# Residual tiles of the attention output projection: from 64 loads of 256 KB into scratch tiles to 16 loads of 1 MB into the query tile

## The reference

```python
x = x + attn(layernorm(x), wq, wk, wv, wo)     # attn ends in  y @ wo
x = x + ffn(layernorm(x), w_gate, w_up, w_down)
```

## Time and profile before

| what | value |
|---|---|
| time before, median of 3 runs | 6593.12 us (6577.72 to 6980.12) |
| the profiled execution's own time | 6586.74 us |
| its span (core 2, the slowest) | 6585.2 us |
| spans of the 8 cores | 6537.8 to 6585.2 us |
| PE busy, share of the span | 5290.5 us, 80% |
| output projection loops of the four slots, core 2 | 541.6 us in sum |

### The profile page before, as it was taken

The page is one execution under the profiler, slowest core; times in us unless marked ns, Lnnn a source line. Parts: engine busy times, 40 slices in busy tenths (PEclk is TensorE's granted clock), DMA queues, the critical chain, the costliest instruction groups (busy, mean ns, idle before and its releaser), DMA issues. The chain is left out here.

```text
span 6585.2 us, 56999 instructions; the slowest of 8 cores (6537.8 to 6585.2 us)
## 1 busy us (share of the span) xinstructions
PE 5290.5 (80%) x21360; PEld 2023.8 (31%) x21360; DVE 996.9 (15%) x1236; ACT 1358.1 (21%) x1451; POOL 310.4 (5%) x382
## 2 busy tenths in 40 slices
PE   5777767647874788558986399999999998888997
PEld 1222222112221222212222144444444443443443
DVE  1222223124112410041000100000000000000000
ACT  1222213312541366115662000000000000000000
POOL 0000000000000000000000010011111110000000
PEclk8777778667886888878887699999999998999999
DMA  7445412022012200310002466666666666667774
GB/s 107 67 74 88 67 37 48 28 86 67 1 32 88 61 1 1 99 56 13 1 1 80 103 96 96 96 96 96 96 96 96 96 96 161 223 230 226 234 233 166
DMA packets 581435, 599.36 MB, mean 91 GB/s; under 512 B 343601, under 2 KB 454194, under 8 KB 581170
## 3 DMA queue, kind: packets, MB, share of 16 engines
q0 software_dynamic: 346016, 272.65, 25.6%
q1 hardware_dynamic: 235154, 323.06, 15.4%
HBM read 625.02 MB, written 125.83 MB: 114 GB/s over the span
## 5 line engine op out<-in xcount | busy, mean ns | idle before, releaser
L1251 PE MATMUL pDa<-gld,wdl 128*128 128x512 bf16 x4096 | 904.7, 385 | 141.9 <-DVE ost L1265 110.4
L1128 PE MATMUL pG<-ln2T,wgb 128*128 128x512 bf16 x4096 | 896.8, 380 | 79.3 <-DMA wub<-wuT 79.3
L1141 PE MATMUL pU<-ln2T,wub 128*128 128x512 bf16 x4096 | 894.5, 379 | 0.0
L880 ACT ACTIVATE probs<-pS,kbb,rsc 128x1024 bf16<-128x1024 f32 (+3 forms) x640 | 729.8, 1140 | 502.0 <-PE pS L853 318.9
L1251 PEld LDWEIGHTS pDa<-gld,wdl 128*128 128x128 bf16 x4096 | 404.7, 99 | 641.9 <-issue 172.0
L1128 PEld LDWEIGHTS pG<-ln2T,wgb 128*128 128x128 bf16 x4096 | 400.9, 98 | 566.0 <-issue 84.0
L1141 PEld LDWEIGHTS pU<-ln2T,wub 128*128 128x128 bf16 x4096 | 401.2, 98 | 482.9
L982 PE MATMUL pY<-lyT,wqb 128*128 128x512 bf16 x1024 | 293.0, 457 | 249.9 <-DMA wqb<-scr_wo 236.1
L894 PE MATMUL pR<-probs,selb 128*1 128x512 bf16 (+3 forms) x1280 | 380.6, 380 | 92.8 <-ACT probs L880 48.0
L1150 ACT ACTIVATE silo<-pG 128x2048 f32<-128x2048 f32 x64 | 120.1, 1877 | 1621.0 <-PE pG L1128 1621.0
L1153 DVE TENSOR_TENSOR gst<-silo,pU 128x2048 bf16<-128x2048 f32 x64 | 146.4, 2288 | 1681.5 <-PE pU L1141 1681.5
(11 more groups left out here) (115 smaller groups left out, 2598.3 us busy)
## 6 DMA issues: line engine op xcount, KB each, us to landing
gld<-scr_gated SPq DMA_DIRECT2D x64, 1024.0 KB, 6.8
wdl<-scr_wd SPq DMA_DIRECT2D x64, 1024.0 KB, 12.3
wdl<-scr_wd POOLq DMA_DIRECT2D x64, 1024.0 KB, 11.2
wgb<-wgT POOLq DMA_DIRECT2D x64, 512.0 KB, 8.6
wub<-wuT POOLq DMA_DIRECT2D x64, 512.0 KB, 15.8
wds<-wdT POOLq DMA_DIRECT2D x64, 512.0 KB, 17.1
scr_wd<-wds SPq DMA_DIRECT2D x64, 512.0 KB, 10.3
scr_gated<-gst SPq DMA_DIRECT2D x64, 512.0 KB, 9.8
```

The lines of the kernel that those rows point to most:

```text
L880: rcol=rcol: e.activation(A(probs[g2], noff, [[1024, 128], [512, 2], [1, 512 - noff]]), A(pS[g2], noff, [[1024, 128], [512, 2], [1, 512 - ...
L1128: ctx.op("tensor", lambda e, dk=dk, gi=gi, buf=buf: e.matmul(pG[:, gi * 512:(gi + 1) * 512], wgb[buf][:, dk * 128:(dk + 1) * 128], ln2T[:, ...
L1141: ctx.op("tensor", lambda e, dk=dk, gi=gi, buf=buf: e.matmul(pU[:, gi * 512:(gi + 1) * 512], wub[buf][:, dk * 128:(dk + 1) * 128], ln2T[:, ...
L1251: pD=pD: e.matmul(pD[:, dki * 512:(dki + 1) * 512], wdl[buf][:, hci * DSW + dki * 128: hci * DSW + dki * 128 + 128], gld[buf][:, hci * 512 ...
```

## The change

Three things are edited, all in `ph_slots`.

- The residual is loaded four blocks at a time, in 4 loads of 1 MB per slot (128 partitions x 4 x 512 f32) and not in 16 of 256 KB. They go into `xr4v`, a view of `qT` as f32 with two halves of 4 blocks, which alternate. The load of a group is issued by SP at the first block of the group (`dk` 0, 4, 8, 12) and stands ahead of that block's weight load. It waits for the last addition that read its half and for the end of attention (`yev`, and `avp` for the first two groups of a slot).
- The waits that guarded `roq0` and `roq1` against residual loads go (one before each rotation, one before the copy in attention); each write of `qT` (L809) gets waits for the residual loads instead.
- In the statistics, a square waits for the casts of its own two blocks and not for that of block 15, and each matmul on `xbq` waits for the cast of its own block; before, only the first had a wait.

```diff
             qT = asb("qT", [128, NH * 512], BF16)
+            xr4v = qT.bitcast(F32)
...
-            xr0 = roq0
-            xr1 = roq1
...
                         ctx.op("vector", lambda e, x1=x1, ro=ro: e.tensor_mul(ro[0:64, :], x1, csq[:, :]),
-                               waits=[("tm", mq["proj"][qc]), ("d_cs", m_cs),
-                                      (f"d_xr{qc % 2}", ctx.c(f"d_xr{qc % 2}"))])
+                               waits=[("tm", mq["proj"][qc]), ("d_cs", m_cs)])
...
                             qT[:, qc * 512:(qc + 1) * 512], ro[:, :], pY[:, 0:512]),
-                            waits=[("tm", m_rqb)])
+                            waits=[("tm", m_rqb),
+                                   ("d_xr0", ctx.c("d_xr0")), ("d_xr1", ctx.c("d_xr1"))])
...
                             ctx.op("vector", lambda e: e.tensor_copy(roq0[:, :], pR[:, 0:512]),
-                                   waits=[("tm", m_rb), ("d_xr0", ctx.c("d_xr0"))])
+                                   waits=[("tm", m_rb)])
...
+                    m_xr4 = {}
                     for dk in range(DK):
                         buf = dk % 2
+                        NXR = min(4, (NH * 256) // 1024)
+                        HWID = NXR * 512
+                        g4 = dk // NXR
+                        if dk % NXR == 0:
+                            xb4 = g4 % 2
+                            ctx.op("sync", lambda e, g4=g4, xb4=xb4, slot=slot: e.dma_start(
+                                out=A(xr4v, xb4 * HWID, [[NH * 256, 128], [512, NXR], [1, 512]]),
+                                in_=A(dram["xqT"].tensor, g4 * NXR * 128 * OWN + slot * 512,
+                                      [[OWN, 128], [128 * OWN, NXR], [1, 512]])),
+                                waits=[("vm", max(mk["xres_v"][xb4], mk["yev"])),
+                                       ("tm", mk["avp"] if g4 < 2 else 0),
+                                       (f"d_xr{xb4}", ctx.c(f"d_xr{xb4}"))],
+                                inc=f"d_xr{xb4}", n=16)
+                            m_xr4[g4] = ctx.c(f"d_xr{xb4}")
                         ctx.op("sync" if buf == 0 else "gp", lambda e, dk=dk, buf=buf: e.dma_start(
...
-                        ctx.op("sync", lambda e, dk=dk, buf=buf, slot=slot: e.dma_start(
-                            out=xr[buf][:, :],
-                            in_=A(dram["xqT"].tensor, dk * 128 * OWN + slot * 512,
-                                  [[OWN, 128], [1, 512]])),
-                            waits=[("vm", max(mk["xres_v"][buf], mk["yev"])),
-                                   (f"d_xr{buf}", ctx.c(f"d_xr{buf}"))], inc=f"d_xr{buf}", n=16)
-                        m_xr = ctx.c(f"d_xr{buf}")
+                        m_xr = m_xr4[g4]
...
-                            o1f[buf][:, :], pO, xr[buf][:, :]),
-                            waits=[("tm", m_o1), (f"d_xr{buf}", m_xr),
+                            o1f[buf][:, :], pO,
+                            xr4v[:, (g4 % 2) * HWID + (dk % NXR) * 512:(g4 % 2) * HWID + (dk % NXR) * 512 + 512]),
+                            waits=[("tm", m_o1), (f"d_xr{g4 % 2}", m_xr),
...
-                            waits=[("sm", m_o1b[DK - 1]), ("tm", m_prb2)])
+                            waits=[("sm", m_o1b[min(DK - 1, (hb + 1) * nb - 1)]), ("tm", m_prb2)])
...
-                                waits=([("sm", m_o1b[DK - 1])] if dk == 0 else []))
+                                waits=[("sm", m_o1b[dk])])
```

More of the change, by code:

```diff
@@ L683, in build_program @@
             o1f = [o1f0, o1f1]
-            xr = [xr0, xr1]
             def ph_slots(ctx):
@@ L988, in ph_slots @@
                         m_o1 = ctx.c("tm")
-                        ctx.op("vector", lambda e, buf=buf, pO=pO: e.tensor_add(
-                            o1f[buf][:, :], pO, xr[buf][:, :]),
-                            waits=[("tm", m_o1), (f"d_xr{buf}", m_xr),
+                        ctx.op("vector", lambda e, buf=buf, pO=pO, dk=dk, g4=g4: e.tensor_add(
+                            o1f[buf][:, :], pO,
+                            xr4v[:, (g4 % 2) * HWID + (dk % NXR) * 512:(g4 % 2) * HWID + (dk % NXR) * 512 + 512]),
+                            waits=[("tm", m_o1), (f"d_xr{g4 % 2}", m_xr),
                                    (f"d_sp{buf}", ctx.c(f"d_sp{buf}")),
                                    ("sm", m_o1b.get(dk - 2, 0))])
-                        mk["xres_v"][buf] = ctx.c("vm")
+                        mk["xres_v"][g4 % 2] = ctx.c("vm")
                         m_add[dk] = ctx.c("vm")
```

## The result

The changed kernel is slower by a little: its time is 1.0063 times that of before, with a 95% interval of 1.0041 to 1.0085. On 6587 us that is +41 us (27 to 56). The forecast was +38 us, 1.0058. In many executions of both kernels the cores of one half of the chip, or of both, ran at a lower clock and some per cent longer, which lifts the plain medians of 11 runs each (6855.02 us before; 7005.88 us after, beyond the predicted range), so ratios compare undisturbed executions alone. The changed kernel took 6617.72 to 6641.12 us in those. All rows after are of core 2, the core shown before; its span is 6602.5 us.

A forecast was written before the change was run, and what follows sets the result against it. The prediction held the output projection bound by issue and landing of transfers, not PE. Per slot 7.1 + 3 x 2.3 - 4 x 0.9 - 0.9 = +9.5 us; four slots, +38 us on 6586.7, so 6625 us; range 6570 to 6695.

The forecast's parts named there:

- The bound and the direction: Output projection: bound by when transfers are issued and land, not by PE; the change would cost +38 us.
- first block of a slot: Block 0: its weights queue behind the residual group on SP and PE waits for both, +7.1 us per slot.
- blocks 4, 8, 12: Projection blocks with a residual group ahead of the weights: PE restarts 10.4 us after POOL's issue, +2.3 us each.
- blocks 2, 6, 10, 14: Projection blocks without a group ahead: the odd addition is no longer late, gap 7.2 us, -0.9 us each.
- block 15's addition: End of each slot's projection: the addition the statistics wait for comes 0.9 us earlier (0 to 1.3).
- PE's clock: Projection matmuls: longer gaps do not slow them, taken as 0 with about 10 us either way.
- the rule: Landing times of DMA transfers: 2.4 us base plus 0.8 us per 256 KB, transfers of all queues added up.
- the blocks hold nothing back: Rival, projection loops: weights land as now beside the group's packets; -14 us, 6573 us; chance 0.20.
- that estimate: Whole kernel, from the skill's page: 48 transfers fewer at a fixed 2 us make 96 us, so 6491 us.
- Slow groups: Rival, residual loads: groups come at the small tiles' pace, 1.4 us per 256 KB; +135 us, 6722; chance 0.09.
- The statistics that overlap after all: Rival, second layernorm's statistics: most of 22 us hidden under the projection, say 20 us per slot, 6545 us; chance 0.03.

The follow-up runs named there:

- the finer waits alone: The kernel before with only the statistics' waits changed to the casts each instruction needs; ratio to before 0.9995 (0.9902 to 1.0088).
- the swapped one: The changed kernel with the weights issued ahead of the residual group in blocks 0, 4, 8 and 12; ratio to before 1.0003 (0.996 to 1.0046).
- the second group: The changed kernel with another 1 MB residual load ahead of the group at blocks 4, 8, 12; no ratio given, mean gap 12.70 us against 10.12.
- the swapped kernel with all weights on POOL: The changed kernel with weights ahead of the residual group and all output projection weight loads issued by POOL; ratio to before 0.9672 (0.9638 to 0.9707).

## Why the prediction was right in its path, and which step failed

**The bound and the direction.** Right: the stage waits for issue and landing, the group ahead of the weights costs more than the odd additions gave, and the loss is in the projection loops. +38 us were forecast and +41 us measured (27 to 56); the loops were to last 580 us and last 583.5. The predicted 6625 us lies among the executions compared, 6617.72 to 6641.12.

**Term by term**, over the four slots of core 2 (gaps counted from POOL's issue, averaged over all pairs of a kind):

| term | forecast, us | measured, us |
|---|---|---|
| first block of a slot, 4 times | +28.4 | +26.3 (6.6 each) |
| blocks 4, 8, 12: gap 8.0 to 10.1, 12 times | +27.6 | +24.9 (2.1 each) |
| blocks 2, 6, 10, 14: gap 7.8 to 6.5, 16 times | -14.4 | -20.2 (-1.3 each) |
| block 15's addition, 4 times | -3.6 | -4.6 (-1.1 each) |
| matmuls, from 293.0 to 308.4 | 0 | +15.4 |
| sum | +38 | +41.8 |

That the sum is so near is luck: the four terms of gaps and of block 15 came out 12 us below their forecast together, and the term put at nothing came out 15 us above it.

**PE's clock.** This is the step that failed: "a longer gap does not show as slower matmuls", taken as 0 with 10 us either way. The matmuls took 15 us more (9 to 20 us on cores 0 to 3), at a stage clock of 0.70 instead of 0.75. Two pairs of the trace before were too few to read this from. In its place the runs show that a matmul takes longer on the whole in the kernels that have the groups in SP's queue beside the weights, whatever their gaps. On cores 0 to 3 the mean of one was 450 to 457 ns before (451 to 461 with the finer waits alone), 465 to 475 in the changed kernel, 460 to 475 in the swapped one, whose gaps on core 2 are no longer than before, and 462 to 467 with the second group, whose gaps reach 12.7 us. (Means are compared because some traces hold 1001 of the 1024 matmuls.) So the length of the gaps alone does not explain it; which part of the new rhythm does stays open.

**The gain of blocks 2, 6, 10 and 14.** This term was too small, -14.4 us for -20. The prediction took the lateness of the odd addition from one pair, 0.91 us, and not from its own mean of 1.3; over the 28 pairs of core 2 the mean is 1.40 us. From the same pair it took 6.4 us from the store's issue to PE's restart, where the mean of the 28 is 5.7 us (4.5 to 7.4). The kernel before, third slot, shows a pair with 1.61 and 4.49 us:

```profile
2741.78 0.53 POOL L964 DMA_DIRECT2D wqb<-scr_wo  x1 [16.44 <-PE pY L982]
2743.39 0.69 DVE L989 TENSOR_TENSOR o1f<-pY,roq 128x512 f32<-128x512 f32 x1 [4.52 <-DMA roq<-xqT]
2744.15 0.32 SPq L996 DMA_DIRECT2D scr_out<-o1f  x1
...
2748.64 9.44 PE L982 MATMUL pY<-lyT,wqb 128*128 128x512 bf16 x32 [7.39 <-DMA wqb<-scr_wo]
```

After the change it is 5.9 us without a group (5.7 in the pair shown, 1330.45 + 0.76 to 1336.92). So taking the small residual tiles away made the weights land no sooner; what fell away is the lateness. With a group, nine units by the rule, 9.6 us were forecast and 9.4 measured (1309.95 + 0.76 to 1320.16).

**The rivals.** That the blocks hold nothing back is refuted: the weights landed behind the group in each slot, and turning the order at the head took PE's wait there away. The fixed cost per transfer of the Trainium skill's rule (SBUF — State Buffer, "The DMA setup-cost knee") did not decide: 48 transfers fewer made the kernel slower, as this cost was hidden but for the odd additions; where the weights had left SP's queue the groups did gain, about half of the 96 us of that estimate. Slow groups: 0.6 to 1.1 us per 256 KB, not 1.4. The statistics that overlap after all: refuted, by the rows of the change and of the finer waits alone.

## What to carry to other kernels

On an engine that issues in order, ask of each transfer what is queued behind its wait: joining small loads into a large one can pay only if nothing urgent stands behind it. Put the loads that the critical engine waits for first, or on a queue in which no store waits for that same engine's results. And a finer wait frees nothing while the instruction still stands behind what it waited for; move the instruction.

## What was not expected of the hardware

PE's mean granted clock went with the rhythm of the stage: 0.75 in the first loop before, 0.70 after, and 0.92 to 0.94 in the four loops of the swapped kernel with all weights on POOL, where PE's idle time before these matmuls is 87.0 us and not 249.9. There a matmul took 402 ns where it took 457 before, so that closing gaps paid twice. And landing times differed by pair of cores within one execution of the swapped kernel, 10.4 us against 8.1 us for the same 1 MB load.
